# Layer 0 of a two-layer graph network: the first eight tiles gathered from x during the node stage, TensorE reading x in place, and gathers up to tile 40 that do not wait for sums

## The reference

```python
# layer 0
x_t = mlp2(x, W1n, b1n, W2n, b2n)                  # per node: 64 -> 128 -> 64, leaky ReLU between
e_t = mlp2(edge_attr, W1e, b1e, W2e, b2e)          # per edge: 32 -> 64 -> 64
agg = segment_sum(x_t[src] * e_t * dp_scale, dst)  # per target node
x = layernorm(x + affine_layernorm(x + agg * res_w))
# layer 1
xw  = einsum(x, rel_w)                             # 8 tables, one for each relation
msg = xw[edge_type, src] * edge_weight
x   = layernorm(x + relu(segment_sum(msg, dst) + h_bias))
```

## Time and profile before

| | us |
|---|---|
| three runs | 4873.51, 4873.86, 4874.02 (median 4873.86) |
| the profiled execution, its own time | 4852.9 |
| its span, from first to last instruction | 4851.1 |
| first gather of layer 0 issued | 74.48 |
| first message of layer 0 | 132.27 |
| tile 40 of layer 0 issued | 330.83 |
| first gather of layer 1 issued | about 2630 |

### The profile page before, as it was taken

One profiled execution on the slowest core, in us unless ns is written; L12 is line 12 of the kernel. 1 busy time (PEld: TensorE's weight loads), 2 busy tenths in 40 slices (PEclk: granted clock), 3 DMA queues, 4 the chain that ended last, 5 costly groups with the idle time before them and its releaser, 6 DMA issues.

```text
span 4851.1 us, 32143 instructions
## 1 busy us (share of the span) xinstructions
PE 1993.1 (41%) x6900; PEld 1435.4 (30%) x6901; DVE 1488.5 (31%) x3786; ACT 303.5 (6%) x628; POOL 2998.0 (62%) x3223
## 2 busy tenths in 40 slices
PE   6545545454555554555554222232222232222322
PEld 5333333333333333333332121121221221222222
DVE  4323333333333333333333222222222222223223
ACT  3000000000101111011111000000000000000000
POOL 6566656655655565555553666766666666666665
PEclk8776666666676676667776555555555555555555
DMA  4111111111111111121111111111111111111111
GB/s 103 31 33 34 34 32 44 33 43 43 44 43 43 42 44 35 43 52 43 49 33 51 24 24 24 25 24 24 25 25 24 25 26 27 25 24 27 27 27 25
DMA packets 199836, 169.83 MB, mean 35 GB/s; under 512 B 83053, under 2 KB 135425, under 8 KB 199523
## 3 DMA queue, kind: packets, MB, share of 16 engines
q0 software_dynamic: 100032, 102.60, 11.9%
q1 hardware_dynamic: 99202, 64.51, 4.5%
q10 hardware_dynamic: 288, 0.07, 0.0%
HBM read 134.87 MB, written 32.10 MB: 34 GB/s over the span
## 4 chain that ended last, share of the span: by engine, by line
another core or an unknown queue 34%; issue 29%; PE 11%; DVE 9%; POOL 8%; DVEq 7%; ACT 2%; ACTq 1%; DMA 0%; SPq 0%; POOLq 0%
POOL rows L641 4%; POOL acc L641 4%; PE ps_agg L1472 3%; DVE acc L1082 2%; PE ps_z L1448 2%; PE ps_o L1464 2%; DVE work L1071 2%; DVE work L1162 2%; ACT low L702 1%; DVEq L1096 1%; DVEq L1082 1%; DVEq L1086 1%; DVEq L1148 1%; DVEq L1061 1%
## 5 line engine op out<-in xcount | busy, mean ns | idle before, releaser
L1472 PE MATMUL ps_agg<-work 128*128 128x192 f32 x2348 | 733.8, 457 | 1711.7 <-DVE work L1162 941.6
L1472 PEld LDWEIGHTS ps_agg<-work 128*128 128x128 f32 x2348 | 551.8, 265 | 1924.1 <-DVE work L1162 987.6
L641 POOL DMA_INDIRECT rows<-rel_table,row_ix x800 | 755.9, 945 | 449.2 <-issue 234.3
L641 POOL DMA_INDIRECT acc<-node_table,acc x763 | 720.6, 944 | 490.9 <-PE ps_agg L1472 235.3
L641 POOL DMA_INDIRECT rows<-node_table,acc x760 | 718.1, 945 | 489.6 <-issue 214.3
L641 POOL DMA_INDIRECT acc<-rel_table,row_ix x763 | 719.7, 943 | 337.3 <-issue 226.3
L1129 DVE SCALAR_TENSOR_TENSOR hid<-ps_z,b1e_c,low 128x512 f32<-128x512 f32 x196 | 147.1, 751 | 1327.1 <-ACT low L702 1014.3
L1082 DVE TENSOR_TENSOR acc<-acc,ps_agg 64x96 f32 x1174 | 288.5, 246 | 824.5 <-remote 644.9
L1071 DVE TENSOR_TENSOR work<-ps_x,rel 128x768 f32<-128x768 f32 x392 | 372.0, 949 | 39.8 <-issue 38.7
L1448 PE MATMUL ps_z<-attrT,W1e_d 128*128 128x256 f32 (+1 forms) x784 | 377.8, 616 | 7.5 <-issue 7.5
L1464 PE MATMUL ps_o<-W2e_d,hid 128*128 128x128 f32 x1564 | 345.9, 390 | 0.0
(11 more groups left out here) (167 smaller groups left out, 1235.9 us busy)
## 6 DMA issues: line engine op xcount, KB each, us to landing
attr<-in_edge_attr_dram SPq DMA_DIRECT2D x39, 640.0 KB
rel_table<-acc SPq DMA_DIRECT2D x19, 1280.0 KB
rows<-rel_table,row_ix POOLq DMA_INDIRECT x800
acc<-node_table,acc POOLq DMA_INDIRECT x763
acc<-rel_table,row_ix POOLq DMA_INDIRECT x763
rows<-node_table,acc POOLq DMA_INDIRECT x760
node_table<-work SPq DMA_DIRECT2D x24, 128.0 KB, 2.0
out_dram<-x_sb SPq DMA_DIRECT2D x19, 160.0 KB
```

Of the source, the lines that this page charges most:

```text
L641: nc.gpsimd.indirect_dma_start(ring[t % RING][0:n, j, :], None, table, bass.IndirectOffsetOnAxis(ap=lists[0:n, t, j : j + 1], axis=0),).th ...
L1472: last = nc.tensor.matmul(bank[:, 0 : 2 * W], data[:, 2 * jj : 2 * jj + 2, :], hot[:, 2 * jj : 2 * jj + 2, :], start=(jj == 0), stop=(jj = ...
```

## The change

It has four parts.

1. `stage` is gone: `node_transpose` reads `x_sb` itself, and the node loop of TensorE is written out. GpSimd does its clears, casts and row numbers apart from the pairs.
2. The ten-tile source list is loaded, cast and turned early (after node pair 3), and GpSimd gathers tiles 0 to 7 of layer 0 from `x` during the node stage. Tile t of these waits until node pair 5t + 4 has its second product.
3. After the lists are turned, the node MLP is run in the ring on the eight gathered tiles: 16 more node pairs (PAIRS to NODES - 1), before the first edge product. `src_turned` is made before the control numbers.
4. The wait for sums begins in layer 0 at tile 40 instead of tile 8. The wait for the slot's message stays.

```diff
+    RAW = 8
+    NODES = PAIRS + RAW * J // 2
+    LISTS_AFTER = 2
+    PAIRS_PER_RAW = (PAIRS - 2 * LISTS_AFTER) // RAW
...
+        def of_gathered(q):
+            t, half = divmod(q - PAIRS, J // 2)
+            return ring[t][:, half * 2 : half * 2 + 2, :]
...
-            def stage(q):
-                if q >= 2:
-                    pool.wait_ge(node_T, q - 1)
-                nc.gpsimd.tensor_copy(
-                    x_pair[:, q % 2, :], x_sb[:, 2 * q : 2 * q + 2, :].rearrange("p b f -> p (b f)")
-                ).then_inc(node_staged, 1)
...
             def gather(l, t):
-                table = (node_table, rel_table)[l]
+                table = (x if t < RAW else node_table, rel_table)[l]
...
+                if l == 0 and 0 < t < RAW:
+                    pool.wait_ge(node_mm2, t * PAIRS_PER_RAW + 2 * LISTS_AFTER)
...
-                if t % V == 0 and t >= V * SUMS_BEHIND:
+                if t % V == 0 and t >= (2 * RING, V * SUMS_BEHIND)[l]:
                     pool.wait_ge(scattered[l][V - 1], t // V - SUMS_BEHIND + 1 + SUM_LEAD)
...
+            for t in range(RAW):
+                if t == CAST_FIRST:
+                    for n in (DST, SRC, TYPE):
+                        for c in range(RCH):
+                            cast(n, c)
+                if t == FORM_FIRST:
+                    for c in range(RCH):
+                        form_rows(c)
+                gather(0, t)
...
+            node_hidden(PAIRS, PAIRS % 2)
+            for q in range(PAIRS, NODES):
+                if q + 1 < NODES:
+                    node_hidden(q + 1, (q + 1) % 2)
+                node_store(q, q % 2)
...
             def node_transpose(q, k):
-                pe.wait_ge(node_staged, q + 1)
-                nc.tensor.transpose(node_psT[k][:, 0:P], x_pair[:, k, :], ident[:]).then_inc(node_T, 1)
...
+                if q >= PAIRS and (q - PAIRS) % (J // 2) == 0:
+                    pe.wait_ge(gathered[0][(q - PAIRS) // (J // 2)], TILE_GATHERS)
+                pair = of_gathered(q) if q >= PAIRS else x_sb[:, 2 * q : 2 * q + 2, :]
+                nc.tensor.transpose(
+                    node_psT[k][:, 0:P], pair.rearrange("p b f -> p (b f)"), ident[:]).then_inc(node_T, 1)
...
+            pe.wait_ge(list_taken, 12)
+            for q in range(PAIRS, PAIRS + 2):
+                node_transpose(q, q % 2)
+            node_first(PAIRS, PAIRS % 2)
+            node_transpose(PAIRS + 2, PAIRS % 2)
+            for q in range(PAIRS, NODES):
+                further_pairs(q, NODES)
```

More of the change, by code:

```diff
@@ L175, in bass_gnn_resnorm_d2_kernel @@
         enorm = sb("enorm", [P, TILES, J])
-        x_pair = rows[:, 0, :, :].rearrange("p (k b) f -> p k (b f)", k=2)
-        first_i = rows[0:BODY, 4:6, :, :].rearrange("p t j f -> p (t j f)").bitcast(i32)
-        first_f = rows[0:BODY, 6:8, :, :].rearrange("p t j f -> p (t j f)")
+        first_i, first_f = (a[0:BODY, 0:P, :].rearrange("p t j -> p (t j)") for a in (row_ix, enorm))
         attrT = sb("attrT", [P, V * P])
-        node_xT = [attrT[:, 0:P], rows[:, 1, 0:2, :].rearrange("p j f -> p (j f)")]
+        node_xT = [attrT[:, k * P : (k + 1) * P] for k in range(2)]
         low = sb("low", [P, 2, 2 * P])
@@ L604, in form_rows @@
                 nc.gpsimd.tensor_tensor(o, o, a, ALU.add).then_inc(rows_formed, 1)
[L606 to L620, removed]
-                if CAST_FIRST + 3 * RCH <= q < CAST_FIRST + 4 * RCH:
-                    form_rows(q - CAST_FIRST - 3 * RCH)
             def gather(l, t):
-                table = (node_table, rel_table)[l]
+                table = (x if t < RAW else node_table, rel_table)[l]
                 if l == 1:
@@ L644, in gather @@
                     ).then_inc(gathered[l][t % RING], 16)
+            for k in range(ZERO_FIRST):
+                zero(k)
+            pool.wait_ge(first_loaded, 16)
+            nc.gpsimd.tensor_copy(first_f, first_i).then_inc(first_cast, 1)
+            for k in range(ZERO_FIRST, ZERO_PARTS):
+                zero(k)
+            for t in range(RAW):
[7 more added lines that the diff above has]
+                gather(0, t)
             for l in range(2):
@@ L651, in _ @@
                     pool.wait_ge(list_taken, 6)
-                for t in range(TILES):
+                for t in range((RAW, 0)[l], TILES):
                     gather(l, t)
@@ L677, in _ @@
             node_copy(1, 1)
-            with act.Fori(0, (PAIRS - 3) // 2) as i:
+            for q in range(2 * LISTS_AFTER):
+                node_lower(q, q % 2)
+                node_copy(q + 2, q % 2)
+            act.wait_ge(first_turned, 1)
+            nc.scalar.copy(
+                src_ix[:, :, :], ps_fin[:, 0 : J * BODY].rearrange("p (j t) -> p t j", j=J)
+            ).then_inc(first_taken, 1)
+            with act.Fori(LISTS_AFTER, (PAIRS - 3) // 2) as i:
                 for k in range(2):
@@ L1370, in _, with further_pairs, turn_first_lists @@
             pe.wait_ge(s_node_const, 16 * len(NODE_CONSTS))
-            with pe.Fori(0, (PAIRS - 3) // 2) as i:
-                for k in range(2):
-                    node_first(i * 2 + (k + 1), 1 - k)
-                    node_transpose(i * 2 + (k + 3), 1 - k)
-                    node_second(i * 2 + k, k)
-            node_first(PAIRS - 2, 1)
-            node_second(PAIRS - 3, 0)
-            node_first(PAIRS - 1, 0)
-            node_second(PAIRS - 2, 1)
-            node_second(PAIRS - 1, 0)
-            pe.wait_ge(first_cast, 1)
-            for j in range(J):
-                last = nc.tensor.transpose(
-                    ps_fin[:, j * BODY : (j + 1) * BODY], first_f[:, j * P : (j + 1) * P], ident[0:BODY, 0:BODY])
-            last.then_inc(first_turned, 1)
+            def further_pairs(q, end):
+                if q + 1 < end:
+                    node_first(q + 1, (q + 1) % 2)
+                if q + 3 < end:
+                    node_transpose(q + 3, (q + 3) % 2)
+                node_second(q, q % 2)
+            def turn_first_lists():
+                pe.wait_ge(first_cast, 1)
+                for j in range(J):
+                    last = nc.tensor.transpose(
+                        ps_fin[:, j * BODY : (j + 1) * BODY], first_f[:, j * P : (j + 1) * P], ident[0:BODY, 0:BODY])
+                last.then_inc(first_turned, 1)
+            for q in range(PAIRS):
+                further_pairs(q, PAIRS)
+                if q == 2 * LISTS_AFTER - 1:
+                    turn_first_lists()
             pe.wait_ge(s_spans, 1)
```

48 lines of the change are left out of this document (27 added, 21 removed).

## The result

The changed kernel takes 4897.31 us (median of 5 runs, 4888.51 to 4901.64) against 4873.86 before: ratio 1.0047, 95% interval 1.0034 to 1.006. It is 23.4 us slower; 4892 was forecast. The profiled execution is the one of 4888.51 us.

The account below looks back on a forecast made before the run. Took TensorE's signals lagging under unbroken gathers, and the gathers themselves, as bounds. First message at 183 plus 163 us to tile 34's makes 346 against 327.5, so 4873.9 + 18.5 = 4892 us; range 4840 to 4918.

Parts of the forecast that it names:

- The reading: Under unbroken gathers TensorE passes 80 to 108 instructions, then about one a us, until gathers are still 4 to 5 us.
- Parts 1 and 2: Node stage with x in place and eight raw tiles: 9 us a held tile, tile 8 at 90 us (80; 102).
- The first rival: Raw tiles don't hold the node stage: tile 8 at 80, first message at 168, +3.5 us, 4877; chance 0.18.
- The 4 us for x in place: Node stage without GpSimd's 49 copies: the table would be ready some 4 us sooner than at 74.48.
- Part 3: Lists and 16 pairs: tile 10 at 107, run to 157, 6 to 8 pairs inside, first message at 183 us.
- Part 4: Ring with sums from tile 40: 163 us from first message to tile 34's, where it was 195.2.
- the sum: First message at 183 plus 163 puts tile 34's message at 346 us, 18.5 later; everything after it as before.
- the rate inside the run: Tiles 10 to 19: TensorE passes 80 to 108 instructions, then 35 to 45 more at about one a us.
- the head start's worth: Ring phase: 12 tiles early are worth 60 us of gathers but only some 32 us, handed back at tile 40.
- The second rival: Signals don't lag in the 16 written-out pairs: first message at 119, tile 34's at 304, -24 us, 4850; chance 0.29.

Follow-up runs that it names:

- experiment 1: Changed kernel with layer 0's wait for sums from tile 8 again: 4879.1 us against 4867.5 before, ratio 1.0025.
- experiment 3: Changed kernel with tile 10's gather waiting until the sixteen further pairs had their second product: 4892.3 us against 4867.5 before, ratio 1.0049.
- experiment 7: Changed kernel with the 32 raw gathers replaced by GpSimd fills and plain DMAs behind them: 4875.9 us against 4846.0 before, 4026.8 against 4038.5.
- experiment 5: Changed kernel without raw tiles and further pairs, sums from tile 8: ratio 1.0005 where before takes 4848.1 us, 1.0001 where it takes 4038.5.
- experiment 2: Kernel before with only layer 0's wait for sums moved to tile 40: 4893.1 us against 4867.5 before, ratio 1.0056.
- experiment 4: Changed kernel without any wait for sums in layer 0: 4904.1 us against 4867.5 before, ratio 1.0067.

## Why the prediction was right or wrong

**The reading** The earlier trace rows holds for the chips on which before takes 4846 to 4874 us, as experiments 1, 3 and 7 show: TensorE's signals come at once without gathers and beside fills and plain DMAs, and late beside indirect ones. It is not a property of the kernel or of every chip. On the others nothing is held, and GpSimd alone is the bound. One part of the reading was not evidence: that the earlier trace rows have a third without an owner. The trace of a lagging chip holds few records of semaphores at all (see below), so "remote" there can mean a missing record. What carries the reading are the starts of the waiting instructions, as in the earlier trace rows.

**Parts 1 and 2.** Tile 8 came at 93.0, where 90 was put (80; 102). A raw tile costs 7.9 to 8.0 us for three of the first four distances and 10.2 for the fourth, against 9. GpSimd's own series is through at 90.4, and the last 2.5 us are the table's. The first rival, that raw tiles hold nothing, had tile 8 at 80 and falls here; on a chip without the lag it is true, 81.5. The 4 us for x in place are not there (experiment 5).

**Part 3.** Tile 10 at 107.7 (107); the run's last gather ends at 157.9 (157); seven pairs inside the run (6 to 8). That the seven came out has luck in it: 57 matmuls and loads pass in the first 10 us of the run, where 80 to 108 were put, and then 96 in 40.2 us, 2.4 a us, where 1.0 was put. Together that is 153, at the end of the 115 to 153 of the forecast. The first message at 189.0 was put at 183: the signals came back 6 us after the run and not 4, and from there to the first edge products at 179.2 it took 15 us and not 12. GpSimd's idle time before tile 20 is 31.7 (26).

**Part 4.** From the first message to tile 34's it is 159.6 us (163), and GpSimd idles 43.2 before tile 40 (45). So the sum was right in its terms, apart from the rate inside the run: 348.6 for 346. From there to the end nothing was to change. The two profiles differ by 14.5 us more, of which 12.2 is the choice of execution.

**The step that failed** is not a term of the sum but what I took it to mean: that the further pairs in the run make the first message late, and the late message the end. Experiment 3 takes the pairs out of the run and has the message 40 us earlier, for the same time. Experiment 2 has no pairs at all and costs 25.6 us. What costs is a long run of indirect gathers in itself, whatever stands in it: 110 to 153 matmuls and loads pass in 50 us of it (experiment 3 and the changed kernel). Why runs broken by GpSimd's pauses, as before, cost less is argued and not shown: each run may let a first lot of instructions pass, as the earlier trace rows has it. No run varied the length of the pauses alone. The parts do not add: sums from tile 40 cost 25.6 us alone, parts 1 to 3 cost 11.6 alone, and together they cost 19.9 to 23.4. I put the head start's worth at 32 of 60 us, and from the first message to tile 34's it is worth just that: 159.6 us against 195.2 before, 35.6 less. Against the kernel with sums from tile 8 it is 37.5. But the run that builds it makes the first message 43.4 us later there (189.0 against 145.6), and in experiment 2 it costs 60.2 and gives back 35.8. After that the lead is worth nothing: the pace is 6.4 us a tile with any lead (experiment 4).

**The second rival**, signals that do not lag in the sixteen pairs, I gave 0.29 and 24 us of gain, by way of written-out code. That reason was wrong: on the lagging chips the written-out pairs are held, and on the others the loops, with all their branches, keep up with the gathers (1749.9 us for 350 tiles). The rule of the Trainium skill, "Runtime: NRT & Kernel Launch", section on instruction fetch mechanics, is that straight-line code is fetched ahead and that a taken branch to a target outside the window stalls. The traces of the lagging chips disagree with it as an explanation of this lag, since 75 matmuls of written-out pairs pass in 50 us. On the others a short stall at a branch could hide behind GpSimd, so they say nothing for or against it. But the outcome that the rival stood for is real: the changed kernel gained 35.8 us on the one faster chip on which it ran, and the kernel with plain DMAs 31.9 us on another. I had treated as a chance of mechanism what is a difference between chips, and the trace of one chip could not tell me.

**What stays open.** What makes a chip lag. Its gathers are issued every 1.25 us, as on the others, and the granted clock is the same on average, 0.63 to 0.64. Packets of the instruction queue between 200 and 2500 us take 0.43 us at the median in the changed kernel on either kind, so slow instruction fetches do not show as the cause. Whether the other cores of the chip play a part was not tried. No chip was met at two different times, so a lasting property of a chip and a state that it was in for a while can't be told apart.

A rival that nothing here tests is the recording itself. On lagging chips the traces hold 14 to 16 thousand records of semaphore updates, on the others 58 thousand, for nearly the same program; of landings of DMAs 10 to 12 thousand against 52 thousand. In the 50 us of forty gathers it is 112 landing records against 630. Outside gathers the records are about as many on either kind: from 20 to 104 us with fills, 1777 and 1758. So on a lagging chip records are lost just where TensorE's signals are late. All times on record come with a span and a granted clock of the profiler, and no run without it stands beside them. The late signals may therefore be a property of such a chip, or of such a chip while it is recorded.

No version here beats before where signals lag; where they don't, the changed kernel itself is the fastest of those run.

## What to carry to other kernels

Before giving a gather engine a head start, look how far the messages stand behind the gathers: 5 to 6 tiles with "remote" waits meant that TensorE's signals were late and a head start was worth nothing, 1.5 tiles that GpSimd was the bound and every early gather worth its full time. Try a change of the order of work on more than one chip before believing its sign: this one is 0.47% slower on one and 0.83% faster on another. Moving a victim out of a disturbed stretch gained nothing here while the stretch stayed as long and other work took the victim's place.

## What was not expected of the hardware

- The same program takes 4846 to 4874 us on some chips and 4038 to 4039 on others, 17% less, at the same mean granted clock.
- Late signals were seen only on such a chip and only beside indirect DMAs in a row. Fills of 1370 elements and 1.28 us each and plain DMAs issued every 0.56 us (32 in 17.8 us) did not bring them.
- On a lagging chip it is TensorE's signals that are late, by up to 3.3 us beside runs of four gathers and by 27 us and more in a run of forty (125.9 to 153.0). What ScalarE hands to VectorE and VectorE to TensorE in the node pairs is taken up within 0.2 us.
- Where signals lag, the profile gives no time from a gather's issue to its landing, because most landing records are missing; on the other chips it gives 2.4 us.
